# Copying a transposed tile out of PSUM: eight casts of every tile pair moved from VectorE to ScalarE

## What is computed

```python
def attn(x):                                   # x has been layer-normalised
    q, k, v = split(x @ Wqkv + bqkv, 3)
    q = q / norm(q); k = k / norm(k)
    kv = sum(k * v, axis=rows)                 # one row of 1024
    return (q * kv) @ Wout + bout

def ffn(x):                                    # x has been layer-normalised
    h = layer_norm(x, ln1_g, ln1_b)
    h = gelu(h @ ternary_quant(w1).T + b1)     # 4096 wide, exact gelu
    h = layer_norm(h, ln2_g, ln2_b)
    return h @ ternary_quant(w2).T + b2

x = x + attn(layernorm(x))
x = x + ffn(layernorm(x))
```

## Time and profile before

| what | value |
|---|---|
| runs shown | 2623.24 and 2716.84 us, median 2670.04 |
| profiled execution, its own time | 2624.99 us |
| its span, slowest core (core 7) | 2623.4 us |
| spans of the 8 cores | 2595.7 to 2623.4 us |
| mean granted TensorE clock, core 7 | 0.816 |
| busy: TensorE, VectorE, ScalarE | 1656.8, 1010.1, 771.5 us |

### The profile page before, as it was taken

The page is one execution under the profiler, slowest core; times in us unless marked ns, Lnnn a source line. Parts: engine busy times, 40 slices in busy tenths (PEclk is TensorE's granted clock), DMA queues, the critical chain, the costliest instruction groups (busy, mean ns, idle before and its releaser), DMA issues.

```text
span 2623.4 us, 35430 instructions; the slowest of 8 cores (2595.7 to 2623.4 us)
## 1 busy us (share of the span) xinstructions
PE 1656.8 (63%) x10928; PEld 914.9 (35%) x10928; DVE 1010.1 (39%) x2702; ACT 771.5 (29%) x1313; POOL 118.0 (4%) x217
## 2 busy tenths in 40 slices
PE   0365564444538135867867867867867867867867
PEld 0122221111213021534534534534534534534544
DVE  0566644444435124243243243243243243243243
ACT  0133346665664000321222222222222212212211
POOL 2111101111110000000000000000000000000000
PEclk9976777676768557878888888888888888888889
DMA  9876535545451780100100100010010010010000
GB/s 145 193 193 199 172 109 162 178 151 178 154 158 57 133 140 15 35 29 21 33 29 21 29 34 21 27 35 21 25 37 21 25 37 21 24 38 21 21 17 17
DMA packets 203594, 195.39 MB, mean 74 GB/s; under 512 B 160404, under 2 KB 160405, under 8 KB 203415
## 3 DMA queue, kind: packets, MB, share of 16 engines
q0 software_dynamic: 31200, 92.34, 13.3%
q1 hardware_dynamic: 157952, 67.18, 10.9%
q10 hardware_dynamic: 14264, 33.62, 3.4%
HBM read 117.55 MB, written 50.33 MB: 64 GB/s over the span
## 4 chain that ended last, share of the span: by engine, by line
PE 50%; DVE 13%; issue 9%; ACT 8%; DVEq 8%; DMA 7%; SPq 4%; POOL 1%; ACTq 1%; POOLq 0%
PE py L677 19%; PE py L718 17%; PE pqkv L578 7%; DMA wstg<-w 5%; PE patt L657 3%; DVEq L949 2%; DVEq L792 2%; SPq L315 2%; SPq L309 2%; DVE outbuf L1033 2%; DVEq L1040 1%; DVE kvtmp L833 1%; ACT qhat L379 1%; DVE xring L954 1%; ACT khat L388 1%
## 5 line engine op out<-in xcount | busy, mean ns | idle before, releaser
L578 PE MATMUL pqkv<-wqkvp,h1T 128*128 128x512 bf16 x1536 | 409.1, 435 | 360.3 <-DVE qkvb L822 331.0
L677 PE MATMUL py<-w2p,h4buf 128*128 128x512 bf16 x2048 | 556.4, 406 | 125.3 <-DVE outbuf L1041 124.0
L718 PE MATMUL py<-z1T,w1p 128*128 128x256 bf16 x4096 | 488.3, 284 | 166.5 <-ACT h4buf L486 164.8
L718 PEld LDWEIGHTS py<-z1T,w1p 128*128 128x128 bf16 x4096 | 386.9, 101 | 268.6 <-issue 171.4
L578 PEld LDWEIGHTS pqkv<-wqkvp,h1T 128*128 128x128 bf16 x1536 | 164.7, 109 | 604.0 <-issue 472.1
L991 DVE TENSOR_TENSOR h4sq<-h4buf 128x128 bf16<-128x128 bf16 x1024 | 222.9, 224 | 305.1 <-PE psumSQ L686 272.7
L486 ACT ACTIVATE h4buf<-py,beta1c 128x256 bf16<-128x256 f32 x512 | 241.1, 474 | 236.3 <-PE py L718 235.8
L1049 DVE CAST z1T<-pzT 128x128 bf16<-128x128 f32 x256 | 56.5, 282 | 568.3 <-PE pzT L698 567.7
L686 PE MATMUL psumSQ<-onesb,h4sq 128*128 128x1 bf16 x1024 | 167.5, 164 | 84.5 <-DVE h4sq L991 84.5
L686 PEld LDWEIGHTS psumSQ<-onesb,h4sq 128*128 128x128 bf16 x1024 | 104.3, 102 | 231.2 <-issue 126.2
L683 PE MATMUL psumSQ<-onesb,h4buf 128*128 128x1 bf16 x1024 | 174.7, 171 | 0.0
(11 more groups left out here) (125 smaller groups left out, 1272.3 us busy)
## 6 DMA issues: line engine op xcount, KB each, us to landing
wstg<-w POOLq DMA_DIRECT2D x128, 512.0 KB, 6.6
xbufA<-x SPq DMA_DIRECT2D x32, 512.0 KB, 5.3
xbufB<-x SPq DMA_DIRECT2D x32, 512.0 KB, 3.6
out<-outbuf ACTq DMA_DIRECT2D x32, 512.0 KB, 2.7
h1scr<-h1buf ACTq DMA_DIRECT2D x32, 256.0 KB, 5.5
qhscr<-qhat ACTq DMA_DIRECT2D x32, 256.0 KB, 2.5
wqkvp<-wqkv POOLq DMA_DIRECT2D x8, 768.0 KB, 27.9
h1T<-h1scr SPq DMA_TRANSPOSE x256, 2.9
```

The lines of the kernel that those rows point to most:

```text
L578: mm = te.matmul(out=pq[i % 4][:, :], lhsT=h1T[:, (g % 2) * 4096 + c * 512 + s * 128: (g % 2) * 4096 + c * 512 + (s + 1) * 128], rhs=wqkvp ...
L677: mm = te.matmul(out=py2[:, hh * 512:(hh + 1) * 512], lhsT=h4m, rhs=w2p[:, m * D + hh * 512:m * D + (hh + 1) * 512], start=(m == 0), stop= ...
L718: mm = te.matmul(out=py1[m % 2][:, :], lhsT=w1p[:, c * H + m * 128:c * H + (m + 1) * 128], rhs=z1T[:, c * 256:(c + 1) * 256], start=(c == ...
```

## The change

The two `zT_evac` calls for tile j0+2 leave VectorE's list. ScalarE gets a function with the same job, `zT_evac_sc`, which waits for the same semaphore, copies with 4 ACTIVATEs of the function Copy and counts the same semaphore up. It is called twice in the loop of the pairs, behind the 32 GELUs and ahead of `sc_tail(j0)`. The casts of tile j1+2 and of the first two tiles stay on VectorE. So 15 pairs have 8 casts moved, 120 of the 256.

```diff
+            def zT_evac_sc(t, r):
+                g = 2 * t + r
+                sc.wait_ge(bzt.h, g + 1)
+                for cc in range(4):
+                    c = 4 * r + cc
+                    cp = sc.activation(
+                        out=z1T[:, c * 256 + (t % 2) * 128:c * 256 + (t % 2) * 128 + 128],
+                        in_=pzT[:, cc * 128:(cc + 1) * 128], func=AF.Copy)
+                bze.inc(cp)
+
             def sc_front(t):
...
                         in_=py1[m % 2][:, :], func=AF.Gelu,
                         bias=beta1c[:, m:m + 1]))
+                if j0 + 2 < NT:
+                    zT_evac_sc(j0 + 2, 0)
+                    zT_evac_sc(j0 + 2, 1)
                 sc_tail(j0)
...
                 if j0 + 2 < NT:
                     dv_front(j0 + 2)
-                    zT_evac(j0 + 2, 0)
-                    zT_evac(j0 + 2, 1)
                 dv_h4sq(j0)
```

## The result

The changed kernel takes 0.9906 of the time of the kernel before, 95% interval 0.9873 to 0.9939: 0.94% faster, or 24.7 us of 2625. That is within 2% and clear of zero. The forecast was 2601.7 us and the profiled execution took 2605.22. Executions in which the cores of a die ran at a lower clock are left out of the ratio: without them the middle of the eight that are left, the profiled one among them, is 2598 us, and with them the plain median of the 14 others is 2652.1 us.

The account below looks back on a forecast made before the run. TensorE's waits on VectorE and ScalarE were taken to bound the kernel. Steps 1 and 2 (7.7 us) plus the clock (15.6) made 23.3 us off 2624.99: 2601.7 us, range 2588 to 2665, likeliest case 2591 to 2612.

Parts of the forecast that it names:

- Step 1: Start of y2(j0): VectorE squares four blocks early, so TensorE's wait for the squares goes; 0.71 us saved a pair.
- Step 2: Between the z1 transpose rounds: four ScalarE copies take 1.03 us plus 0.05 against 0.88 on VectorE; 0.20 us lost a pair.
- Step 3: TensorE behind the second transpose round: the drops to 1.2 GHz go, at 1.3 us each; 15.6 us (8.6 to 19.1).
- 12 falls: Of 15 boundaries y1 to y2(j0), those with granted clock 0.50 to 0.55 behind the wait for the squares.
- The lower bound of 0.72: Lower price in us of one clock drop, from round to round of the next pair: 99.04 against 98.32.
- A: Rival: behind the second transpose round the clock falls as before, only steps 1 and 2 count; 2617.3 us, chance 0.15.
- B: Rival: ScalarE's copies take as long as a GELU (474 ns), nothing is gained; 2625 us, chance 0.05.
- C: Rival: a 1.28 us table load precedes ScalarE's first copy, between the rounds; 2640.5 us, chance 0.06.
- D: Rival: copies run at their lower bound and no clock gain is given back; 35.6 us saved, 2589.4 us, chance 0.04.

Follow-up runs that it names:

- e1: Kernel before with the first four squares of j0 ahead of the casts in VectorE's list, all casts staying on VectorE; ratio 0.9884, pair 97.49 us.
- e2: Changed kernel, but VectorE waits for both copied rounds before its first square of j0; ratio 0.9989, pair 98.97 us.
- e4: Changed kernel with nine extra 32-column scratch copies of round 0 on ScalarE ahead of the real ones; ratio 0.9989, pair 98.97 us.
- e8: Kernel before with an unused early Sqrt on ScalarE, taking the table load out of the tail of j0; ratio 0.9982, pair 98.69 us.
- e6: Changed kernel with an unused early Sqrt on ScalarE behind the copies, ahead of the tail of j0; ratio 0.9803, pair 95.53 us.
- e5: Changed kernel with the second transpose round of j0+2 issued inside y2(j0), ahead of block 3; ratio 0.9806, pair 95.56 us.
- e9: Kernel before with four squares of j0 ahead of the casts and the unused early Sqrt, no copies on ScalarE; ratio 0.9799, pair 95.54 us.
- e10: e7 with ScalarE writing z1 of j0+2 behind the pair's fourth GELU instead of ahead of the first; ratio 0.9619, pair 92.17 us.
- e3: Changed kernel with three extra 128-column scratch copies of round 0 on ScalarE ahead of the real ones; ratio 0.9944, pair 97.99 us.
- e7: Changed kernel with the edits of e5 and e6 together; ratio 0.9785, pair 95.28 us.

## Why the prediction was right, and where not

*Step 1, the squares.* Right to the hundredth: 1.07 us from the second round to block 1, 0.71 saved a pair. e1 shows it alone.

*Step 2, the copies.* The sign was wrong. I took 338 ns for a copy, between the one-column ACTIVATE and the GELU; it takes 284 ns (the ACTIVATE group z1T<-pzT, 120 times, 23.6 us), and four take 0.79 us instead of 1.03. The line between the two rows was too steep: the GELU's time holds more than its columns. It has a bias operand and the copy has none, but no run shows whether that is the reason. The 0.05 us for a slower start did not show either. So the copies give 0.10 us a pair where I had a loss of 0.20; steps 1 and 2 together are 12.2 us and not 7.7. The figure of the Trainium skill (ScalarE: Activation LUTs, "What ACT_TABLE_LOAD costs") gives 293 ns and 0.89 us for four; the run agrees within 9 ns for one and lies 0.10 us below it for four.

*Step 3, the clock.* The mechanism was right: without the late squares all 12 falls go (e1), with them they come back (e2), and a longer single wait brings them back too (e4). The price was not. I took 1.3 us a fall out of 0.72 to 1.59; 10.9 us for 12 falls are 0.9 each (1.1 by the busy time). The rest is given back behind the waits for j0's output and for the GELUs in every other pair. The lower bound of 0.72 had this in it already, but it was read the wrong way round: of the two pairs compared it is the later one, without a fall, that met more time at 1.2 GHz further on, as the first 20 us of y2(j1) show (the earlier pair, then the later):

```profile
1225.64:1245.64 20.00, 14.96 (x105) 0.75 0.07 27
1620.41:1640.41 20.00, 14.96 (x98) 0.72 0.07 27
```

The two errors, 4.5 us too little for steps 1 and 2 and 4.7 too much for the clock, cancel, and that is luck: 23.1 us in the pairs against 23.3.

*What bounds the kernel.* One sentence was wrong, though the forecast did not suffer from it: "a microsecond taken out of one of these waits should shorten the pair by a microsecond". e8 takes 1.28 us out of such a wait in each pair and the time stays the same within its interval; e6 takes the same 1.28 us out and the pair falls by 1.9.

*The rivals.* A (the clock falls as before) is refuted: 0 of 15. The rule of the Trainium skill behind it (TensorE: Matmul & The Clock Gate, "Why this matters for your kernels") doesn't hold for this place, since waits of 1.84 us already bring the lower clock in 14 of 15 pairs (e4). B (copies as slow as GELUs) fell with the 284 ns. C (a table load ahead of the copy) fell too: the table loads are 16 for the GELUs and 16 for the Sqrt, as before, and the copies have none, which agrees with the Trainium skill (ScalarE: Activation LUTs, "Table sets: the hidden batching unit"). D's lower bound of the copies was not reached, and of the clock's 19.1 us 10.9 came.

*What stays open.* No run shows why the pair is held at just these lengths, or at what idle time between 1.54 and 1.84 us the clock begins to fall at this place.

## What to carry to other kernels

When an engine stands at a wait with ready work behind it, look at that work: here four squares that could have been done long before cost TensorE 0.7 us a pair, and moving them ahead on their own engine gave all that moving the casts to another engine gave. After that, read TensorE's granted clock behind each of its waits before pricing the wait: a short one can double the time of the matmuls that follow, and in a loop whose length is held by such stretches one edit gives nothing (e8) and the same edit, combined with another, more than its own length (e6). So try small edits together as well as one by one.

## What the runs showed that I had not expected

In this loop, the mean length of a pair takes few values. Four kernels with different waits stand at 98.97 or within 0.3 us of it (before 98.98, e2 98.97, e4 98.97, e8 98.68 to 98.92 by core), three at 95.5 (e5 95.56, e6 95.53, e9 95.54), one at 92.17 (e10), 3.4 us apart; the changed kernel, e1 and e3 lie between and change from pair to pair between about 96.3 and 99. Kernels with the same length differ by up to 1.3 us in the waits of a pair, and slower matmuls make up the difference. The 14 pairs of e8 (core 6), of e6 and of e7:

```profile
1101.80:2483.30 1381.50, 1042.04 (x7840) 0.85 0.09 28
1102.39:2439.76 1337.37, 1008.24 (x7842) 0.87 0.09 29
1103.01:2436.92 1333.91, 1020.39 (x7843) 0.86 0.09 29
```

e8 has 1042.0 us of matmuls in 1381.5 us, where the kernel before has 1028.5 us for as many in 1385.7 us. e7 has one wait of 1.03 us a pair less than e6, and 12 us more of matmuls. In both, most of what the shorter wait saved went into slower matmuls.
